# Where the attention weighing and two value fills stand in a batch's eight places

## The reference, cut to what matters

```python
q = split_heads(query @ Wq.T + bq)          # 64 queries a batch, 16 heads of 16
k = split_heads(bank @ Wk.T + bk)           # 1601 keys a batch
v = split_heads(bank @ Wv.T + bv)
attn = softmax(q / 4 @ k^T)
ctx = attn @ v                              # "weighing" in this kernel
x = x + ctx @ Wo.T + bo
```

## Time and profile before

| | |
|---|---|
| median of 3 runs | 2118.18 us (2115.8 to 2119.51) |
| time of the profiled execution | 2124.54 us |
| its span | 2122.7 us |
| PE matmul busy | 1970.8 us, 93% |
| DVE busy | 1287.4 us, 61% |
| ACT busy | 1050.8 us, 50% |
| POOL busy | 672.6 us, 32% |
| mean granted PE clock | 0.986 |

### The profile page before, as it was taken

The page is one execution under the profiler, slowest core; times in us unless marked ns, Lnnn a source line. Parts: engine busy times, 40 slices in busy tenths (PEclk is TensorE's granted clock), DMA queues, the critical chain, the costliest instruction groups (busy, mean ns, idle before and its releaser), DMA issues.

```text
span 2122.7 us, 72750 instructions
## 1 busy us (share of the span) xinstructions
PE 1970.8 (93%) x31780; PEld 1587.3 (75%) x31796; DVE 1287.4 (61%) x2276; ACT 1050.8 (50%) x1532; POOL 672.6 (32%) x1349
## 2 busy tenths in 40 slices
PE   6799999999999999999999999999999998999987
PEld 4577777777778787787878778787777777777764
DVE  3555656756656665766656575665656666565644
ACT  3444455555465555455555544555544444444441
POOL 4323333423233332333324233342323232122301
PEclk8999999999999999999999999999999999999999
DMA  5533434343333343434333425242342321213122
GB/s 185 183 126 119 146 118 137 104 136 126 123 118 116 120 134 107 133 114 151 121 116 129 134 86 169 74 164 90 113 143 86 119 70 62 78 50 107 50 72 70
DMA packets 124472, 243.92 MB, mean 115 GB/s; under 512 B 13952, under 2 KB 44800, under 8 KB 124160
## 3 DMA queue, kind: packets, MB, share of 16 engines
q1 hardware_dynamic: 123568, 239.23, 34.4%
q10 hardware_dynamic: 592, 0.04, 0.0%
HBM read 235.94 MB, written 3.15 MB: 113 GB/s over the span
## 4 chain that ended last, share of the span: by engine, by line
PE 75%; DVE 9%; ACT 7%; issue 5%; POOL 2%; DMA 0%; SPq 0%; POOLq 0%; DVEq 0%; ACTq 0%
PE M L816 12%; PE M L823 11%; PE SC L1034 10%; PE SC L1057 8%; PE O L1078 7%; PE X L873 5%; ACT probT L1280 4%; DVE mx L1623 3%; PE SC L1050 3%; PE M L873 3%; PE X L1144 2%; PE M L917 1%; PE X L852 1%; PE M L878 1%; PE X L1118 1%
## 5 line engine op out<-in xcount | busy, mean ns | idle before, releaser
L1623 DVE TENSOR_REDUCE mx<-SC 128x4 f32<-128x1600 f32 (+1 forms) x256 | 466.9, 1824 | 159.5 <-PE SC L1034 156.0
L1280 ACT ACTIVATE probT<-SC 128x2048 f32<-128x2048 f32 (+1 forms) x256 | 398.8, 1558 | 160.6 <-PE SC L1057 160.1
L656 POOL TENSOR_TENSOR rowsT<-raw,rowsT 128x256 fp32r<-128x256 f32 (+1 forms) x512 | 324.1, 664 | 380.4 <-ACT rowsT L1334 380.3
L823 PE MATMUL M<-wvs,rowsT 128*128 128x256 f32 x2496 | 359.3, 293 | 3.3 <-issue 1.8
L816 PE MATMUL M<-rowsT,wks 128*128 128x400 f32 (+1 forms) x1536 | 341.5, 363 | 9.5 <-issue 3.6
L1219 ACT ACTIVATE kT<-M,bk 128x400 f32<-128x400 f32 (+1 forms) x256 | 151.7, 594 | 379.7 <-PE M L816 379.3
L816 PEld LDWEIGHTS M<-rowsT,wks 128*128 128x128 f32 x1536 | 271.3, 191 | 83.5 <-issue 67.4
L823 PEld LDWEIGHTS M<-wvs,rowsT 128*128 128x128 f32 x2496 | 315.7, 192 | 23.6 <-issue 3.5
L1425 DVE TENSOR_TENSOR V<-M,bv 128x512 f32<-128x512 f32 (+1 forms) x224 | 145.4, 649 | 283.5 <-PE M L823 275.3
L1034 PE MATMUL SC<-kT,bdq 32*128 32x400 f32 (+1 forms) x2048 | 246.6, 550 | 27.6 <-ACT probT L1280 23.2
L1078 PEld LDWEIGHTS O<-probT,V 128*17 128x17 f32 x13312 | 193.7, 99 | 81.6 <-issue 77.0
(11 more groups left out here) (275 smaller groups left out, 2441.3 us busy)
## 6 DMA issues: line engine op xcount, KB each, us to landing
ring<-in_ws_dram SPq DMA_DIRECT2D x428, 256.0 KB, 4.4
summed<-in_ctx_dram SPq DMA_DIRECT2D x60, 800.5 KB, 4.6
raw<-in_ctx_dram SPq DMA_DIRECT2D x64, 384.0 KB, 4.4
raw<-in_ctx_dram SPq DMA_DIRECT2D x32, 512.0 KB, 4.3
ring<-rounded_scratch SPq DMA_DIRECT2D x64, 256.0 KB, 3.8
raw<-in_ctx_dram SPq DMA_DIRECT2D x32, 321.0 KB, 4.4
out_dram<-x SPq DMA_DIRECT2D x16, 128.0 KB, 2.5
kT<-in_ctx_dram SPq DMA_DIRECT2D x2, 800.5 KB, 8.9
```

The lines of the kernel that those rows point to most:

```text
L656: ins = pool.tensor_tensor(rowsT[1][:, c, part], raw[:, c, part], rowsT[0][:, c, part], ALU.subtract)
L823: mm = pe.matmul(bank[:, (t - 2 * a) * D:(t - 2 * a + 1) * D], rowsT[xp][:, cc, t * P:(t + 1) * P], wvs[wp][:, cc, :], start=(at == cc == ...
L1280: act.activation(probT[step % 3][0:w, :, 0:len(ts), :].rearrange("p j t q -> p j (t q)"), SC[0:w, :, 0:len(ts) * P], ACT.Exp)\
L1623: dve.tensor_reduce(mx[c][:, :, n], SC[:, :, 0:KCH[n][1]], AX.X, ALU.max).then_inc(max_used, 1)
```

## The change

At places 2 and 6 `weigh` stands before `maxima` in PE's order, where it stood behind. Value(6) goes from the first half of place 2 to that of place 3, value(0) from the first half of place 3 to the second half of place 2, and value(3) from the first half of place 6 to its second half. The first halves of places 2 and 6 are empty of key and value pieces then. ACT's and DVE's drains follow the lists too. PIECES, `splits` and all else stay.

```diff
-FIRST = [[[value(4)], [value(5)], [value(6)], [value(0)], [key(0, 3)], [value(1)], [value(3)], [value(2)]],
-         [[value(4)], [value(5)], [value(6)], [value(0)], [key(0, 3)], [value(1)], [value(3)], [value(2)]]]
-SECOND = [[[key(0, 0)], [key(0, 1)], [], [key(0, 2)], [key(1, 0)], [key(1, 1)], [], [key(1, 2), key(1, 3)]],
-          [[], [key(0, 0), key(0, 1)], [], [key(0, 2)], [], [key(1, 0), key(1, 1)], [], [key(1, 2), key(1, 3)]]]
+FIRST = [[[value(4)], [value(5)], [], [value(6)], [key(0, 3)], [value(1)], [], [value(2)]]] * 2
+SECOND = [[[key(0, 0)], [key(0, 1)], [value(0)], [key(0, 2)], [key(1, 0)], [key(1, 1)], [value(3)], [key(1, 2), key(1, 3)]],
+          [[], [key(0, 0), key(0, 1)], [value(0)], [key(0, 2)], [], [key(1, 0), key(1, 1)], [value(3)], [key(1, 2), key(1, 3)]]]
...
-WEIGH_FIRST = ()
+WEIGH_FIRST = (2, 6)
```

## The result

The changed kernel takes **2264.52 us** (median of 5 runs, 2258.12 to 2270.58) against 2119.51 us of the kernel before in the same session: a ratio of 1.0684 with a 95% interval of 1.0666 to 1.0703. That is 145 us slower, where I had forecast 84 us slower and a range up to 2240. The sign was right and the size was not.

A forecast was written before the change was run, and what follows sets the result against it. PE, with matmuls in flight 93% of the span, was taken as the bound, so only its idle time counts. Places 98 us plus bank 32, less 40 and 6, gave +84: median 2202 us, range 2158 to 2240.

The forecast's parts named there:

- Place 2, even: Place 2 takes 7.00 us in even batches, 0.72 more, since value(0) doesn't fill DVE's reduce; 7.83 in odd, 1.55 more.
- Place 3, the blocked cast: ACT's cast waits for value(6), delaying exp and PE's maxima at place 3: 1.03 us more in even batches, 0.78 in odd.
- The bank: At place 3, value(6) waits for DVE's drain of value(0), queued behind the division: 17 batches x 1.9 = 32 us.
- Place 6: pw waits for the convolution, 8.55 us, 1.9 more (1.6 taken), in even batches; xq for L1748, 7.13, 0.85 more, in odd.
- The sum of idle time: Places 2, 3 and 6 give 98 us, with the bank 130; less 40 is 90, less 6 given back is +84.
- 14 us of exp waits: PE's waits for exp before the maxima, beyond 0.30 us counted per batch, vanish: 23.2 - 9 = 14 us.
- 27 + 32 - 9 = 50: Place 3's growth: blocked cast 27 us, bank wait 32, less 9 where layer 0's pieces cover the wait for exp.
- rival 5: Clock falls to lower level for 7 us in each of 17 bank-wait batches: up to 119 us more, 2320; chance 0.03.
- rival 2: Only waits of single batches come, no bank wait, much of the rest is given back: +42, 2160 us; chance 0.15.
- 1 and 4: 1: faster, exp waits vanish, others hidden, 2098 us, chance 0.03; 4: no change, idle time absorbs shifts, 2118, chance 0.02.
- (3): Delays go on: POOL's low part comes late, key(0, 3) waits at place 4, 34 us more, 2236; chance 0.15.

The follow-up runs named there:

- The candidate pair: Kernel before with value(0) moved to place 2's, value(6) to place 3's first half; ACT's cast at end of place 2: 2142.7 us, behind place 3's exp: 2112.6 us.
- weighing first alone: The kernel before with only the weighing put in front of the maxima at places 2 and 6, piece lists unchanged: 2210.4 us, ratio 1.0427.

## Why the prediction was wrong, by its steps

- **Place 2, even: right.** 7.00 forecast, 7.01 in batch 28. Odd: 7.83 forecast, 2056.53 - 2048.68 = 7.85 in batch 29, with `gow` 0.74 late. Two small errors cancel in the even one: the rows give 1990.82 - 1987.93 = 2.89 from maxima to the next scores and not 2.95 (measured 2.90), and the part before the maxima took 4.11 instead of 4.05.
- **Place 3, the blocked cast: right in even batches.** Maxima forecast 3.07 into the place, they start 3.12 into it (2003.90 - 2000.78). In odd batches `ff_in` was said to lie in the wait. It does not: it waits itself, for DVE's `rb` in four batches (3, 15, 19 and 29) and for the copy mT in five (5, 13, 21, 25 and 27), and in batch 29 the maxima start 3.51 into the place (2060.04 - 2056.53). The candidate pair confirms by an experiment that the blocked cast costs what was forecast and more.
- **The bank: right.** Up to 2.3 us forecast, 1.9 in the mean of 17 batches; the waits of L822 for L1424 are 1.17 to 2.09 us long (2.08 in batch 16) and sum to 32.2 us, where 32 was forecast. I had missed one batch, 25, where a piece of the experts makes a wait of 0.66.
- **Place 6: right.** 8.55 forecast for batch 30 and 8.55 measured there, 8.39 in batch 28; odd 7.13 forecast, 2089.76 - 2082.67 = 7.09 in batch 29.
- **The sum of idle time: near, partly by luck.** 90 less 6 for what is given back is 84; measured +79.0 in batches 1 to 30, and 224.5 - 151.9 = 72.6 in the whole span. One term of it was misread: 14 us of exp waits beyond those already counted were to vanish. At places 2 and 6 there were only 10.0 us of them before, 9 of which were counted, and 0.4 after; the rest of the 23.2 stood at other places and in batch 0, and stayed. Place 3 makes up for it: 27 + 32 - 9 = 50 us longer was forecast, and without the 40 of slower matmuls it is 30 longer. I can't say which cover there was counted too low.
- **The step that failed** is the sentence "Matmul time hardly changes when pieces only trade places, so the change can win or lose only by PE's idle time", and with it rival 5, the clock, at a chance of 0.03. Busy time grew by 42.8 us in batches 1 to 30 and by 60.7 in the whole, because the granted clock fell to its lower level in 35 stretches instead of 14. I had taken from the earlier trace rows that it held through waits of 1 to 2 us. The row averages 53 us a slice; the kernel before had 14 such stretches, which I would have seen in the mean clock of 0.986 or in finer windows. So the sentence of rival 5 that the trace has no such fall behind its short waits does not hold, as it was read from too coarse a row: three of the 14 begin in a place 3, and in batch 7 the clock fell 0.9 us behind a wait of 1.76 us. Rival 5 named the mechanism and the place, at a price of up to 119 us for all 17 batches. 12 of the batches with a bank wait fell, several of them (4, 7, 9, 11) with this one wait and no second, and so did batches with one wait of 1.7 us, as batch 30.
- The Trainium skill, "TensorE: Matmul & The Clock Gate", HAM oscillation, was cited there as a warning that recurring idle gaps send the clock down and back. The runs agree with its direction: with matmuls put into place 3's waits the mean clock is 0.972 instead of 0.958.
- **Rivals 1 to 4** did not occur. The bank wait came (rival 2), the time is not near 2098 or 2118 (1 and 4), and no wait was added before key(0, 3) at place 4, whose length changed by -2.1 us in 30 batches (3).

Still open is why one place 3 keeps the clock and its twin does not (batches 28 and 30), and why the waits before the B fills of places 2 and 6, mostly 0.8 to 1.6 us, cost the clock so little where those of 1.95 us behind the maxima cost more. No run here separates the length of a wait from what stands around it.

## What to carry to other kernels

When an order list is changed, look for every wait that names a piece by where it used to be filled: here a cast on another engine waited for value(6), and its queue held up the exp. Before taking a piece away from the front of a place, ask which late inputs it had been hiding (a scan, a convolution, a quantization). Price a new wait on PE in two parts, the idle time and the clock behind it: here 79 us of idle time in batches 1 to 30 brought another 42.8 of slower matmuls, and 60.7 counted over the whole span. Half of the time added at the low level gives this price from the trace, without an experiment.

## What the runs showed of the hardware that I had not expected

- The same place with the same 1.73 us wait took 7.04 us with the granted clock at 1.00 and 10.05 us at 0.66.
- In place 3 of batch 30 the clock fell from 2.4 to 1.2 GHz while PE stood for 1.73 us, and in other batches it held through a wait of 2.08 us (1, 16, 18, 23).
- In all eleven kernels without extra matmuls the change in busy time is half of the change in time at the low level, within 6 us (+42.8 and +42.7 for the change).
- Added matmuls made a kernel faster: 144 of them in front of the transposed maxima, and 42 behind value(6), won 32 us (2264.5 to 2232.4). Others in the waits of places 2 and 6 won 6 us, no more than the spread.
- +26.6 us of waits at place 6, mostly 0.8 to 1.6 us long, left the clock at 0.983; 56.3 us more of waits of up to 1.95 us at places 2 and 6 (weighing first alone) took it to 0.973, with 18.5 us of busy time; the change took it to 0.958.
